# Keys of the next sequence turned, stored and fetched three steps sooner; one-hot scalings spread over the steps; the first blocks' keys fetched behind the rotary transfers

## The reference, cut to what matters

```python
def grouped_attention(qt, kvt, kv_mask, v_scale, out_scale, qnorm_g, cnorm_g, null_kv, w_q, w_kv, w_out):
    ...
    k = jnp.concatenate([nk, k], axis=3)
    v = jnp.concatenate([nv, v], axis=3)
    ...
    sim = jnp.einsum('bghqd,bghkd->bghqk', q, k) * DIM_HEAD ** (-0.5)
    sim = jnp.where(kmask[:, :, None, None, :], sim, NEG)
    attn = jax.nn.softmax(sim, axis=-1)
    o = jnp.einsum('bghqk,bghkd->bghqd', attn, v)
    ...
summed = jnp.zeros((Bq, W, d), x.dtype).at[rows, flat_idx].add(flat_out)
...
return summed / jnp.maximum(counts[..., None], 1e-05)
```

## Time and profile before

| | |
|---|---|
| Median of three runs | 744.65 us (743.94 to 745.68) |
| Profiled execution | 741.73 us, its span from first to last instruction 739.9 us |
| PE busy | 679.9 us (92%) |
| DVE busy | 485.4 us (66%) |
| ACT busy | 403.4 us (55%) |
| POOL busy | 258.6 us (35%) |
| Mean granted TensorE clock | 0.992 of full speed |

### The profile page before, as it was taken

How to read it: one execution, slowest core, us unless ns; L and a number is a source line. 1 busy time by engine, 2 the same in 40 slices (tenths; PEclk the granted TensorE clock), 3 DMA queues, 4 the chain that set the end, 5 groups by cost and what they waited for, 6 DMA issues and landing times.

```text
span 739.9 us, 16674 instructions
## 1 busy us (share of the span) xinstructions
PE 679.9 (92%) x5792; PEld 545.6 (74%) x5792; DVE 485.4 (66%) x1045; ACT 403.4 (55%) x1484; POOL 258.6 (35%) x382
## 2 busy tenths in 40 slices
PE   4899999999999899899999999996999989798785
PEld 3678888878887677677777777885878868677574
DVE  6433333349888588668778787657867767666672
ACT  3444444442222466586776767765666666555761
POOL 2130000000001589776758775115444422414110
PEclk9999999999999999999999999998999999999999
DMA  8702000000000332333333334105455444343432
GB/s 250 312 1 63 1 0 0 0 0 0 0 1 2 84 85 61 104 89 91 88 76 74 90 80 94 52 12 190 142 168 168 152 155 159 126 143 132 140 115 64
DMA packets 66618, 65.98 MB, mean 89 GB/s; under 512 B 12368, under 2 KB 52400, under 8 KB 65904
## 3 DMA queue, kind: packets, MB, share of 16 engines
q1 hardware_dynamic: 60320, 45.90, 22.7%
q0 software_dynamic: 6224, 19.14, 7.4%
HBM read 29.50 MB, written 18.61 MB: 65 GB/s over the span
## 4 chain that ended last, share of the span: by engine, by line
PE 58%; DVE 12%; ACT 8%; POOL 5%; SPq 5%; DMA 5%; issue 5%; DVEq 1%; POOLq 1%; ACTq 0%
PE ps L845 9%; PE ps L833 9%; PE ps L1160 7%; ACT stage L1388 6%; PE ps L1135 5%; DVE stage L1743 4%; PE ps L1144 4%; PE ps L820 4%; PE ps L1094 4%; PE ps L814 4%; SPq L526 3%; PE ps L894 3%; DMA stage<-krows 2%; POOL early L661 2%; PE ps L1004 2%
## 5 line engine op out<-in xcount | busy, mean ns | idle before, releaser
L1456 ACT ACTIVATE early<-ps,nmC 128x128 f32<-128x128 f32 (+1 forms) x224 | 77.4, 358 | 68.7 <-DVE nmC L1851 68.7
L642 POOL TENSOR_TENSOR early<-stage 128x512 f32<-128x512 f32 x64 | 87.9, 1394 | 57.4 <-DVE stage L1743 44.8
L1388 ACT ACTIVATE stage<-ps,nmB 128x128 f32<-128x128 f32 x256 | 89.9, 379 | 18.9 <-DVE nmB L1776 18.0
L845 PE MATMUL ps<-stage 128*128 128x128 f32 (+2 forms) x448 | 86.2, 321 | 1.2 <-DVE stage L1637 1.2
L833 PE MATMUL ps<-stage,early 128*128 128x128 f32 (+2 forms) x448 | 86.4, 321 | 0.0
L833 PEld LDWEIGHTS ps<-stage,early 128*128 128x128 f32 x448 | 65.2, 192 | 24.4 <-issue 15.5
L845 PEld LDWEIGHTS ps<-stage 128*128 128x128 f32 x448 | 65.5, 191 | 12.1 <-issue 1.9
L1632 DVE COPY stage<-ps 128x512 f32<-128x512 f32 x32 | 22.1, 691 | 70.0 <-PE ps L820 69.6
L1333 ACT ACTIVATE stage<-ps 128x512 f32<-128x512 f32 x64 | 31.4, 490 | 65.2 <-PE ps L833 65.2
L1395 ACT ACTIVATE stage<-ps 128x512 f32<-128x512 f32 x64 | 35.0, 595 | 51.2 <-PE ps L1004 51.2
L1848 DVE TENSOR_REDUCE nmC<-ps 128x4 f32<-128x512 f32 (+1 forms) x56 | 35.9, 641 | 40.6 <-PE ps L1135 40.6
(11 more groups left out here) (217 smaller groups left out, 1465.0 us busy)
## 6 DMA issues: line engine op xcount, KB each, us to landing
early<-early SPq DMA_DIRECT2D x256, 64.0 KB, 2.0
early<-prows SPq DMA_DIRECT2D x128, 64.0 KB, 2.1
prows<-stage POOLq DMA_DIRECT2D x24, 256.0 KB, 2.6
prows<-early POOLq DMA_DIRECT2D x24, 256.0 KB, 2.6
cos<-prows SPq DMA_DIRECT2D x64, 64.0 KB, 2.1
krows<-stage POOLq DMA_DIRECT2D x8, 320.0 KB, 3.3
stage<-krows SPq DMA_DIRECT2D x32, 80.0 KB, 2.6
x<-in_x SPq DMA_DIRECT2D x4, 256.0 KB, 3.7
```

The costliest lines, as they stand in the source:

```text
L642: pool.tensor_tensor(to, a, b, (ALU.subtract, ALU.add)[f]).then_inc(rot_in, 1)
L845: t = pe.matmul(ps[:, b, q0:q1], vN[:, b % 2, m, :], simA[:, b % 2, s, at:at + q1 - q0], start=False, stop=False, skip_group_check=True)
L1388: t = act.activation(pB[:, u % 2, at, :], ps[:, 4 + h, i * P:(i + 1) * P], ACT.Exp, bias=nmB[:, u % 2, at:at + 1], accum_out=rsB[:, u % 2, ...
L1456: act.activation(pC[:, n % 2, hg, 0:m], ps[:, 5 + k, hg * P:hg * P + m], ACT.Exp, bias=nmC[:, k, hg:hg + 1], accum_out=rsC[:, k, hg:hg + 1])
```

## The change

1. `keys_turned(it + 1)` moves from step 4 to step 1 on DVE, `save_keys(it + 1)` from step 5 to step 2 on POOL, and `place_keys(it + 1)` from behind `place_probs` of step 4 to behind that of step 1 on SP.
2. `scale_picks` handles one block at a step, in steps 0 to 5 of sequences 4 and 5 and steps 0 to 3 of sequence 6; PE waits for 16 increments instead of 2.
3. The fetch of `XT0` moves from behind `place` of `j == 3` to behind the last `place`, ahead of `place_keys(0)`.

```diff
@@ SP
                     place(j, qk, a)
-                if j == 3:
-                    sp.wait_ge(keys0_saved, 16)
-                    keys_first(XT0[:].rearrange("p h b c -> p h (b c)"), k0rows, 4, xt0_placed)
...
+            sp.wait_ge(keys0_saved, 16)
+            keys_first(XT0[:].rearrange("p h b c -> p h (b c)"), k0rows, 4, xt0_placed)
             place_keys(0)
             for n in range(STEPS):
                 place_probs(n)
                 it, w = divmod(n, WQ)
-                if w == 4 and it + 1 < G * B:
+                if w == 1 and it + 1 < G * B:
                     place_keys(it + 1)
@@ POOL
-                    t = pool.tensor_scalar(at, at, rcnt[:, c % BLK, c // BLK:c // BLK + 1], None, ALU.mult)
-                t.then_inc(ohq_scaled, 1)
+                    pool.tensor_scalar(at, at, rcnt[:, c % BLK, c // BLK:c // BLK + 1], None,
+                                       ALU.mult).then_inc(ohq_scaled, 1)
...
-                if w == 5 and it + 1 < G * B:
+                if w == 2 and it + 1 < G * B:
                     save_keys(it + 1)
...
-                if w == 3 and it in (B + 1, B + 2):
-                    scale_picks(8 * (it - B - 1), 8)
+                if it >= B and w < 6 and 6 * (it - B) + w < NB:
+                    scale_picks(6 * (it - B) + w, 1)
@@ PE
-                        pe.wait_ge(ohq_scaled, 2)
+                        pe.wait_ge(ohq_scaled, NB)
@@ DVE
-                if w == 4 and it < last:
+                if w == 1 and it < last:
                     keys_turned(it + 1)
```

## The result

The changed kernel takes 725.52 us (four runs, 722.5 to 727.33); the kernel before, on the same chip, 744.68. The ratio is 0.9724, interval 0.9688 to 0.9761: 19.2 us less by the medians, 20.5 by the ratio, where 16.2 were forecast. The profiled execution takes 724.45 us (span 722.6), 17.3 less than that of before; its mean granted clock is 0.993.

The account below looks back on a forecast made before the run. PE was taken to bound the kernel, with 58% of the last-ending chain. Terms -10.8 + 1.8 + 0.2 - 5.8 - 1.6 = -16.2 us took the median 744.65 to 728.4 us, range 724.5 to 734.

Parts of the forecast that it names:

- keys' fetch: Part C, scores of step 2: fetching keys behind step 1 on SP removes all six waits for `krows`, -10.8 us.
- turning on DVE: Step 1 of sequences 1 to 6: turning keys there makes DVE 0.45 late, costing PE some 0.3 each, +1.8 us.
- sequence 0: Sequence 0, where PE waits for ACT: POOL also clears a buffer and the turning moves, +0.2 us (-0.5 to +0.75).
- scalings: POOL, one scaling a step: PE's projection waits of 2.92 and 2.91 us in sequences 5 and 6 go, -5.8 us.
- first blocks' keys: Part B: the later fetch lets rotary transfers go sooner, the ninth limited by `add(9)`, -1.6 us (0 to -3.3).
- median above the profiled execution: Last step of the sum: the median of runs, 2.9 us above the profiled execution, was kept as the base.
- DVE takes the stall over: Rival: each of the six sequences pays the turning's whole 0.75 us, giving 731.1 us; chance 0.15.
- More comes back: Rival: DVE's lateness costs nothing and part B gives 3.3 us, giving 724.9 us; chance 0.10.
- The wait moves to the mix: Rival: step 4's probabilities land 1 us later than taken, half the keys' gain goes, 733.8 us; chance 0.07.
- A port lock: Rival: eleven scalings on POOL each hold DVE for 0.62 us by the shared-port rule, 735.2 us; chance 0.03.
- SP is blocked: Rival: SP waits for a late `krows` write ahead of later reads, slower than before, 749.5 us; chance 0.05.
- It doesn't do what it says: Rival: SP is held at step 1, keys still late, 10.8 us stays, 739.2 or 737.4 us; chance 0.02.

Follow-up runs that it names:

- a_keys: Kernel before with only the keys' part of the change: turned in step 1, stored in step 2, fetched behind step 1; 735.32 us, ratio 0.9871.
- h_after: The changed kernel measured once more, beside the kernel before on the same chip; 725.23 us, ratio 0.9756.
- b_picks: Kernel before with only the scalings changed, one block a step; 735.16 us, ratio 0.9894.
- c_xt0: Kernel before with only the first blocks' keys changed, fetched behind the last rotary transfer; 740.34 us, ratio 0.9957.
- i_fill: Kernel before with PE kept busy in three waits: repeated mask products before unit 8's scores, 12 idle products before two projections; 742.53 us, ratio 1.0001.
- i2_fill: As i_fill, but 6 instead of 12 idle products ahead of each of the two projections; 741.63 us, ratio 0.9934.
- d_sp3: Kernel before with one line changed: SP fetches the next keys behind step 3 instead of step 4; 733.5 us, ratio 0.9844.
- e_sp3_all: Changed kernel, but keys turned in step 4, stored in step 5 and fetched behind step 3; 722.82 us, ratio 0.9719.
- k_busy: e_sp3_all with extra idle PE products in waits of step 4, step 7 (sequences 0 and 1) and the last sequence; 719.01 us, ratio 0.9649.

## Why the prediction came short

| term | forecast | measured | from |
|---|---|---|---|
| keys' fetch | -10.8 | -11.9 | 6 x (27.33 - 25.34) |
| turning on DVE | +1.8 | +2.6 | 6 x (25.77 - 25.34) |
| sequence 0 | +0.2 | +0.6 | start of part C to step 2 of sequence 1, 29.66 to 30.27; the clock differs there too (0.62 at 504 to 508 us in after, none in before), and `a_keys`, without that stretch, has 28.82 |
| scalings | -5.8 | -6.1 | 30.35 and 30.40 less 27.33 each |
| first blocks' keys | -1.6 | -2.5 | part B as a whole |
| sum, profiled execution | -16.2 | -17.3 | traces: -17.3 too, with part A 0.8 longer, which nothing in the change explains, the last distance 0.5 and the end 0.3 shorter |
| median above the profiled execution | 2.9 | 1.1 | 744.65 - 741.73, 725.52 - 724.45 |

**The step that failed** is the last of the sum: "The median of the runs shown is 2.9 above that execution". It was carried over as a constant. How much is missing isn't sharp: 2.9 us by the medians, 4.3 by the ratio, 2.0 by the ratio of `h_after`, whose interval (15.1 to 21.1 us of gain) holds the 16.2 that were forecast. Behind the change the median is 1.1 above the profiled execution, and in `h_after` 0 (both are 725.23), so 1.8 or more of the 2.9 us are there; the other 1.1 are the sizes in the table. What the runs show in its place is the clock behind PE's waits, which the sum put at nothing. The profiled execution of before had the loss behind its wait in part B, but not behind its two waits for the scalings (3.29 in both the earlier trace rows), where 3 of 8 such waits were followed by it. The waits for `krows` can bring it too. Of the 30 in the five traces that have them (before, `b_picks`, `c_xt0`, `i_fill`, `i2_fill`) it came behind two, one of them this wait of `i2_fill`, with a granted clock of 0.57 from 604 to 608 us and a distance of 29.57 where before has 27.39:

```profile
603.15 1.27 PE L1136 MATMUL ps<-stage,early 128*128 128x128 f32 x8 [2.13 <-DMA stage<-krows]
```

A median over executions holds some of these losses, and the change takes the waits away and the loss with them. An estimate from these counts: two waits at 3 in 8 and 1.6 us, and six at 2 in 30 and 2.2 us, make 2.1 us a run, near the 1.8; from so few counts it gives a size and no more. That the losses can be won without ending a wait sooner is shown by `i2_fill`.

This much stays open. How often the loss comes in the unprofiled runs of before isn't seen directly; their mean clock goes with their time (five runs at 0.992: 739.96 to 741.73; ten at 0.985: 743.75 to 746.02; one each at 0.977 and 0.976: 751.66 and 750.67), and the profiled one is at 0.992. And the mean clock of the runs of `a_keys`, `b_picks` and `d_sp3` (0.985 to 0.987) is not above that of before on the same chip (0.986), though they have fewer long waits; only that of `c_xt0` is (0.992). Their traces have slow stretches between 684 and 696 us, in the last sequence, that the profiled execution of before has not.

**The first blocks' keys.** The wait went from 3.35 to 1.72, so the -1.6 of the wait was right, as was its cause, the ninth transfer behind `add(9)`: in the kernel after SP waits 2.6 for POOL and issues it at 305.42, when `add(9)` has just ended (302.88 and 2.51). The 1.58 behind the wait came on top and was not priced, although the scores' 1.98 stood in the trace. Only 0.9 of it is left at the end of part B; where the rest goes wasn't followed.

**The keys' fetch.** Mechanism and place right: no wait of the scores, and the mix of step 4 doesn't take it over, since the slack of 1.0 held. Each sequence gives 2.0 instead of the wait's 1.8; 0.1 of the difference is the scores themselves, 1.16 behind the wait and 1.05 without. But less had to be moved than the change moves: by `d_sp3` SP's fetch alone, and that by one step, does it all.

**The turning.** DVE is 0.5 behind PE's scores, as worked out (0.45). Of the two slacks of ACT's copies the projection's was right (0.16 lost against 0.25 taken), and the other wrong: the copy of the expanded queries, which ends at 579.86, was put down as having "more slack for its reader", and there PE loses 0.23. The reader stood in PE's timeline of the kernel before, 0.35 behind the end of the copy, hardly more than the 0.2 of the other:

```profile
580.21 1.68 PE L1094 MATMUL ps<-early,G 128*128 128x224 f32 x8
```

**The rivals.** *DVE takes the stall over* would be 0.75 a sequence and was 0.43. *More comes back* was half right, in part B and not on DVE. *The wait moves to the mix*: two short waits for `prows`, 0.9 the longest, both behind 700 us at the end, where before has three (0.9 the longest). *A port lock*: the multiplication beside the scaling of 603.04 takes its 0.69, as do the two others of the trace that overlap a scaling, so the rule that stood behind this rival does not show for this pair of instructions. *SP is blocked*: it issues the keys 3.7 us after POOL's write is issued, and the mix has all it needs. *It doesn't do what it says* fell with the waits.

## What to carry to other kernels

When a transfer is late though its data lay ready long before, look at its place in the queue and at what the instruction ahead of it waits for, and try moving the fetch alone, which cost nothing here, before moving the work that feeds it. Price a wait of TensorE by the distance to the next like piece of work, not by the wait alone, and look at the granted clock behind it. Take the median, not one profiled execution, as the base only after asking what differs between executions, because a change can remove that too.

## What was not expected of the hardware

**The clock behind short waits.** In a kernel whose PE is busy 92% of the span, single waits were followed by a stretch at 1.2 GHz: in part B in all four traces that have the wait unfilled (2.8 to 3.6 us of idle, a loss of 1.5 to 1.6), ahead of the projections behind 3 of 8 waits of 2.9 to 3.1 (1.5 to 1.7), and in sequence 0 behind shorter ones. The same wait of 1.94 for ACT was followed by it in `e_sp3_all`:

```profile
502.55 2.66 PE L1093 MATMUL ps<-early,G 128*128 128x224 f32 x8 [1.94 <-ACT stage L1437]
```

and not in before:

```profile
504.18 1.78 PE L1094 MATMUL ps<-early,G 128*128 128x224 f32 x8 [1.94 <-ACT stage L1438]
```

Behind the 1.72 in part B of the kernel after there was none. With idle products in the wait it did not come (`i_fill`, `i2_fill`, `k_busy`). The Trainium skill (TensorE: Matmul & The Clock Gate, Part 1: The HAM clock gate) says that the array's clock has these two states, that the lower one is the default, and that activity releases it. The traces agree in the two states and in what activity does: 0.65 behind the idle 3.35 us, 1.00 with that wait partly filled. That the lower state is the default they don't show: in the first 8 us, with PE idle, the granted clock of before reads 1.00.

**A DVE multiplication beside an addition on POOL.** In part B of `c_xt0` PE waited for DVE and ACT in the units from 288 to 320 us, which then follow each other in 7.9 to 8.2 us instead of the 7.0 to 7.1 of most units; this hides what part 3 gives. POOL's timeline there:

```profile
294.72 2.94 POOL L641 TENSOR_TENSOR early<-stage 128x512 f32<-128x512 f32 x2 [0.31 <-issue]
```

DVE's:

```profile
294.73 1.80 DVE L1783 TENSOR_TENSOR stage<-stage,riB 128x512 f32<-128x512 f32 x1
```

PE's:

```profile
298.26 0.66 PE L1003 MATMUL ps<-ident,stage 128*128 128x128 f32 x4 [0.49 <-DVE stage L1783]
```

The multiplication that starts just behind the addition takes 1.80 instead of 0.69, 1.11 more, and PE waits 0.49 for it. In the kernel after, whose additions come at other moments, 7 of 64 such multiplications take over 1.2, in `c_xt0` 13. The Trainium skill (SBUF: State Buffer, section SBUF: two separate sides) says that of such two the one that starts first keeps the shared port pair for its whole instruction and the other waits. By that the 1.11 is the rest of an addition, and these rows agree. By the same rule the scaling, which reads one tensor and a column of factors, would hold the multiplication up too, and there the rows differ: 0.69 and 0.70 beside it, as without it. Whether the second tensor makes the difference was not tried.
